# End of the attention: the first tile's rows split two batches sooner, the first product's chunks spread from the last batch's steps 6 and 7 on, Wo loaded a batch sooner

## The chip, the cores and the metric

One core of one Trainium2 chip runs the whole program in one launch. The metric is the device time of that core in microseconds (us), the median over several runs. The kernel before has 1077.09 us (three runs, 1075.11 to 1077.19).

## What is computed

Cut to what matters here (32 batches, 32 query rows and 257 context rows each, width 1024, 32 heads that share 8 key and value heads):

```
x = x + xattn(layernorm(x), context, context, Wq, Wk, Wv, Wo)   # softmax(q k^T / sqrt(32)) v, then @ Wo
x = x + attn(layernorm(x), eta)                                  # within a batch, 32 x 32
x = x + ffn(layernorm(x), gate_w, expert_w)                      # 8 experts, the best 2 of each row
```

Everything is float32. The large products run on TensorE with operands split into a high and a low part; three passes (high*high, high*low, low*high) are added.

## The kernel before

The program has two parts, `attend` and `finish`. In each of them every engine has its own list of instructions, written out by hand, and engines wait for each other by semaphores. There is no planner: the order in which the loops emit the work is the order on each engine. The names: PE is TensorE, ACT ScalarE, DVE VectorE, POOL GpSimd, SP the queue that issues most DMAs.

`attend` runs B + 2 = 34 stages `b` of 8 steps `s`. Three batches overlap: in stage b the keys and values of batch b are projected (`keys` L713, `values` L722), the heads of batch b - 1 are scored (L850), and the last heads of batch b - 2 are finished. A step works on one group of heads. PE makes the scores; DVE takes the maximum (L631); ACT takes the exponentials (L485); DVE takes the reciprocal and scales (L621, L623); two steps later PE turns the shares (`turn_prob`, L761, for the eighth head also L763); ACT or DVE, by a list (`turned_by_scalar`), copies them out of PSUM (L272). There is one PSUM buffer for turned shares, so each turn waits for the copy before it. In step 2 PE multiplies the shares of batch b - 2 by the values (`times_values`, L780), and in step 3 ACT copies the result into `oT` (L502). `oT` holds 8 tiles, each of 4 batches, turned as the product with Wo needs it; the first tile is complete once batch 3 is.

The projections of batch 31 end in step (31, 5). From step (31, 6) on there is nothing to project: these are the short steps, (31, 6) to (33, 3). There PE also makes the first tile's product with Wo, one chunk of 128 rows at a time (`first_product`, L750, six matmuls of 512 columns; steps from `product_step`). A chunk needs both parts of its Wo chunk: ACT makes the high part (L516) in the step of `wo_step`, DVE the low part (L653) one step later. It also needs both parts of the first tile's rows: ACT L520 in step (32, 1), DVE L658 in step (32, 2). The same two lines split the second tile's rows in step (33, 4). The parts lie in `rows`, where keys and shares of batch 30 lay before; thus the waits for `s_done` and `turned`.

SP loads Wo chunks 0 to 2 before stage 28, chunks 3 to 6 after the loop over the stages (they take the place of the context's parts of batch 30, so SP waits for `v_done`), chunk 7 and the two tiles of x for `finish` (L350) behind them. In every stage it stores the keys (L332) and loads them back in another layout (`kcat`, L338). The parts of chunks 3 to 6 take the place of the key and value weights, so ACT waits for the last values.

`finish` starts on each engine as soon as its part of `attend` is over. SP waits for the last `times_values` (`pv_done`), loads the gate four times (L1029, packets of 32 bytes), eta, and the eight chunks of the first expert (L1019). ACT splits the rows of tile 2 (`ot_high`, L1215), then the first expert chunk (`first_high`, L1248), then copies the turned y of tile 0 (`copy_y`, L1222). PE makes the product of tile 1 (`product`, L1546, eight units) with turns of y (L1558) before unit 4 and the small products of rows (`products_of_rows`, L1570) before unit 6; the latter wait for `copy_y`. DVE adds x to the product (`add_x`, L1330), which frees the two banks for the next tile. POOL writes constants first, once `pv_done` is reached.

The lists that the diff changes:

```
wo_step:      ((B - 2, 2), (B - 2, 6), (B - 1, 2), (B, 4), (B, 6), (B + 1, 0), (B + 1, 1), (B + 1, 2))[c]
product_step: ((B, 3), (B, 4), (B, 5), (B, 6), (B + 1, 0), (B + 1, 1), (B + 1, 2), (B + 1, 3))[c]
```

Of the kernel before, what the change touches and what calls it, by code (L numbers as in the profile page):

```python
# [12 lines left out]
ALU = mybir.AluOpType  # L13
ACT = mybir.ActivationFunctionType
# [6 lines left out]
P = 128  # L21
# [33 lines left out]
class Shared:  # L55


    def __init__(self, nc, ctx):
        sb = lambda *a: ctx.enter_context(nc.sbuf_tensor(*a))
        self.sem = sem = lambda n: ctx.enter_context(nc.semaphore(n))  # L60
        self.ident = sb("ident", [P, P], F32)
        self.base = base = nc.sbuf_base
        sb("shared_map", [P, 4 * SLOT + 4 * D], F32)
        self.at = lambda name, offset, shape, dtype=F32: nc.alloc_sbuf_tensor_at(name, shape, dtype, offset=base + offset)
        self.wkv = [self.at("wkv_" + part, HIGH1 + i * SLOT_BYTES // 2, [P, KC, 2 * KV], F32R) for i, part in enumerate("hl")]
        self.cx = self.at("cx", STAGE, [P, 2, 2, D])
        self.oT = self.at("oT", HIGH0, [P, NT, KC, P])
        place = lambda c: LOW1 + 8 * D * (c + 1) if c < EARLY_WO else LOW1 if c == KC - 1 else HIGH1 + 8 * D * (c - EARLY_WO)
        self.wo = [[self.at(f"wo_{part}{c}", place(c) + i * 4 * D, [P, D], F32R) for c in range(KC)] for i, part in enumerate("hl")]
        self.rows = [self.at("rows_" + part, STAGE + 16 * D + ROWS_AT + i * 8 * D, [P, 2, D], F32R) for i, part in enumerate("hl")]  # L70
        self.ot = [part[:, :, :].rearrange("p a (c n) -> p a c n", n=P) for part in self.rows]
        self.x_in2 = self.at("x_in2", STAGE, [P, 2, D])
        self.x2_loaded = [sem("x2_loaded0"), sem("x2_loaded1")]
        self.ot_h_ready, self.ot_l_ready, self.xo_done = sem("ot_h_ready"), sem("ot_l_ready"), sem("xo_done")
        self.w = [self.at("w_h", HIGH0, [P, 2 * SLOT], F32R), self.at("w_l", LOW0, [P, 2 * SLOT], F32R)]
        self.banks = [ctx.enter_context(nc.psum_tensor(f"bank{i}", [P, 512], F32)) for i in range(8)]

        self.chunk_loaded = [sem(f"chunk_loaded{c}") for c in range(KC)]
        self.s_done, self.pv_done = sem("s_done"), sem("pv_done")
        self.block = ctx.enter_context(nc.Block(no_gpsimd_drain=True))  # L80
        self.cx_loaded = [sem("cx_loaded0"), sem("cx_loaded1")]
# [79 lines left out]

def wo_step(c):

    return ((B - 2, 2), (B - 2, 6), (B - 1, 2), (B, 4), (B, 6), (B + 1, 0), (B + 1, 1), (B + 1, 2))[c]


def product_step(c):

    return ((B, 3), (B, 4), (B, 5), (B, 6), (B + 1, 0), (B + 1, 1), (B + 1, 2), (B + 1, 3))[c]


def attend(nc, sh, x, wq, wk, wv, wo, context, q_dram, k_dram, vlast_dram):
# [4 lines left out]
    with ExitStack() as ctx:  # L177
# [97 lines left out]
        def _(sp):  # L275
# [44 lines left out]
            def load_wo(c):  # L320
                sp.dma_start(wo_raw[c][:, :], wo[c * P:(c + 1) * P, :]).then_inc(chunk_loaded[c], 16)

            for b in range(B):
                par = b % 2
                if b == B - 4:
                    for c in range(EARLY_WO):
                        load_wo(c)
                load_context(b)
                sp.wait_ge(klast_ready, 2 * b + 2)
                for part, ready in enumerate((kT_h_ready, kT_l_ready)):  # L330
                    sp.wait_ge(ready, b + 1)
                    sp.dma_start(k_dram[part, par], kT[part][:, par, :, :].rearrange("p j n -> p (j n)").bitcast(F32)).then_inc(k_stored[part], 16)  # L332
                if b >= 2:
                    sp.wait_ge(s_done, NG * (b - 1))
                for part in range(2):
                    sp.wait_ge(k_stored[part], 16 * b + 16)
                    for c in (part, part + 2):
                        sp.dma_start(kcat[par][c * DH:(c + 1) * DH, :, :].rearrange("d (g j) n -> d g (j n)", g=4).bitcast(F32),  # L338
                                     k_dram[part, par].rearrange("(g d) n -> d g n", g=4)).then_inc(kcat_loaded[par], 16)
                if b == 0:  # L340
                    store_q(3)
            sp.wait_ge(v_done, B - 1)
            for c in range(EARLY_WO, KC - 1):
                load_wo(c)
            for part in range(2):
                sp.wait_ge(k_stored[part], 16 * B)
            load_wo(KC - 1)
# [59 lines left out]
        def _(act):  # L407
# [67 lines left out]
            for b in range(STEPS):  # L475
                project, next_one, heads, rest = stage(b)
                par = b % 2
                for s in range(NG):
# [30 lines left out]
                    for c in range(KC):  # L509
                        if wo_step(c) == (b, s):  # L510
# [3 lines left out]
                                act.wait_ge(k_stored[0], 16 * B)  # L514
                            act.wait_ge(chunk_loaded[c], 32)
                            act.activation(wo_s[0][c][:, :], wo_raw[c][:, :], ACT.Copy).then_inc(wo_h_ready, 1)  # L516
                    if (b, s) in ((B, 1), (B + 1, 4)):
                        t = b - B
                        act.wait_ge(s_done, NG * (B - 1))
                        act.activation(sh.ot[0][:, t, :, :], oT[:, t, :, :], ACT.Copy).then_inc(sh.ot_h_ready, 1)  # L520

        @block.vector
        def _(dve):
# [101 lines left out]
            for b in range(STEPS):  # L625
                project, next_one, heads, rest = stage(b)
                par = b % 2
                for s in range(NG):
                    if heads:
                        dve.wait_ge(s_done, NG * (b - 1) + s + 1)  # L630
                        dve.reduce_max(nmax[:, 1 - par, s:s + 1], s_ps[s % 2][:, 0:SK], AXX, negate=True).then_inc(max_done, 1)  # L631
                    if next_one and s in (2, 4, 6):
                        context_low(b + 1, s // 2)
                    if s == 0 and 1 <= b and next_one:
                        context_low(b + 1, 0)
                    if s == 0 and rest:
                        normalize(b - 2, NG - 1)
                    if s >= 1 and heads:
                        normalize(b - 1, s - 1)
                    i = (s - 2) % NG  # L640
                    a = b - 2 if s < 2 else b - 1
                    if s == 2 and project:
                        if b >= 2:
                            dve.wait_ge(k_stored[1], 16 * b - 16)
                        dve.wait_ge(kT_h_ready, b + 1)
                        dve.tensor_tensor(kT[1][:, par, :, 0:2 * P], k_ps[:, :].rearrange("p (j n) -> p j n", j=2),
                                          kT[0][:, par, :, 0:2 * P].bitcast(F32), ALU.subtract).then_inc(kT_l_ready, 1)
                    if i not in turned_by_scalar(a) and (rest if s < 2 else heads):
                        copy_turned(dve, dve.tensor_copy, a, i)
                    for c in range(KC):  # L650
                        if wo_step(c) == (b, s - 1):
                            dve.wait_ge(wo_h_ready, c + 1)
                            dve.tensor_tensor(wo_s[1][c][:, :], wo_raw[c][:, :], wo_s[0][c][:, :].bitcast(F32), ALU.subtract).then_inc(wo_l_ready, 1)  # L653
                    if (b, s) in ((B, 2), (B + 1, 4)):
                        t = b - B
                        dve.wait_ge(turned, NG * (B - 1))
                        dve.wait_ge(sh.ot_h_ready, t + 1)
                        dve.tensor_tensor(sh.ot[1][:, t, :, :], oT[:, t, :, :], sh.ot[0][:, t, :, :].bitcast(F32), ALU.subtract).then_inc(sh.ot_l_ready, 1)  # L658

        @block.tensor  # L660
        def _(pe):
# [80 lines left out]
            def first_product(k):  # L742

                if k == 0:
                    pe.wait_ge(sh.ot_l_ready, 1)
                    pe.wait_ge(cT_l_ready, 4 * B)
                pe.wait_ge(wo_l_ready, k + 1)
                for h in range(2):
                    for m, (a, b) in enumerate(PASSES):
                        o = pe.matmul(banks[h][:, :], sh.ot[a][:, 0, k, :], wo_s[b][k][:, h * 512:(h + 1) * 512],  # L750
                                      start=(k == 0 and m == 0), stop=(k == KC - 1 and m == 2))
                    if k == KC - 1:
                        o.then_inc(sh.xo_done, 1)
# [129 lines left out]
def finish(nc, sh, x, eta, gate, expert_w, out, n_dram, slot_dram):  # L883
# [6 lines left out]
    with ExitStack() as ctx:  # L890
# [320 lines left out]
        def _(act):  # L1211
# [29 lines left out]
            def first_high(e, *chunks):  # L1241
                for c in chunks:
                    if e == 0:
                        act.wait_ge(ot_l_ready, c + 1)
                    else:
                        act.wait_ge(xo_done, 2 * NT)
                    act.wait_ge(chunk_loaded[c], 48 + 16 * e)
                    act.activation(w[0][:, e * SLOT + c * D:e * SLOT + (c + 1) * D], first_raw[e][:, c, :], ACT.Copy).then_inc(w_h_ready, 1)  # L1248
# [498 lines left out]
```

## Time and profile before

| | |
|---|---|
| median of three runs | 1077.09 us (1075.11 to 1077.19) |
| the profiled execution, its own time | 1080.17 us |
| its span | 1078.6 us |
| PE, PE weight load, DVE, ACT, POOL busy | 97%, 89%, 58%, 44%, 23% |
| granted TensorE clock, mean over the span | 0.991 |
| HBM read, written | 148.66 MB, 44.56 MB |

Times within the profile count from the start of the span. A matmul's row shows when it starts and how long it takes from its start to its last result; matmuls overlap, so the pace is the distance from start to start. In brackets stands how long the engine was idle before the row, and what ended it. A granted clock of 1.00 is 2.4 GHz, one of 0.50 is 1.2 GHz.

### The profile page before, as it was taken

The numbers are of one execution on the slowest core, as the hardware profiler recorded it, in microseconds if no ns is written. First come the engines' busy times: TensorE is split into PE (matmuls) and PEld (weight loads), VectorE is DVE, ScalarE is ACT, GpSimd is POOL, SyncE is SP. The second block draws the span as 40 slices with busy tenths as digits, with TensorE's granted clock in tenths as the row PEclk, the third lists the DMA queues.
The fourth block names the chain that finished last, engine by engine and source line by source line (L and its number), as shares of the span: only waits on it lengthen the run. The fifth ranks groups of instructions, "written<-read, shape, count | busy, mean of one in ns | idle before, by whom it ended". The sixth has DMA issues, their size and how long they took to land.

```text
span 1078.6 us, 25384 instructions
## 1 busy us (share of the span) xinstructions
PE 1048.2 (97%) x9043; PEld 957.5 (89%) x9044; DVE 630.6 (58%) x1623; ACT 478.4 (44%) x1129; POOL 243.1 (23%) x412
## 2 busy tenths in 40 slices
PE   8999999999999999999999999799998999999996
PEld 8999999999999999999999998677776778888885
DVE  6641366666666666676766667677778344354220
ACT  4321255555555555555555555522324244454331
POOL 2000212121212111121212121035454223322232
PEclk9999999999999999999999999899998999999999
DMA  9424576566565657575757745365536677578332
GB/s 345 138 79 155 179 243 191 175 181 181 175 197 170 200 164 205 153 213 157 197 161 197 232 145 150 129 240 82 105 128 235 179 231 260 143 242 259 94 77 38
DMA packets 78604, 189.46 MB, mean 176 GB/s; under 512 B 16513, under 2 KB 27137, under 8 KB 74401
## 3 DMA queue, kind: packets, MB, share of 16 engines
q1 hardware_dynamic: 64096, 154.15, 45.7%
q0 software_dynamic: 14400, 33.88, 12.9%
q8 instruction: 69, 1.13, 0.5%
q14 instruction: 39, 0.31, 0.1%
HBM read 148.66 MB, written 44.56 MB: 179 GB/s over the span
## 4 chain that ended last, share of the span: by engine, by line
PE 89%; DMA 5%; DVE 3%; issue 1%; ACT 1%; POOL 1%; POOLq 0%; SPq 0%; DVEq 0%; ACTq 0%
PE bank L1700 17%; PE bank L713 17%; PE bank L722 16%; PE bank L674 9%; PE bank L1546 6%; PE bank L761 6%; PE bank L705 5%; PE bank L780 4%; PE bank L850 3%; DMA xg<-n_scratch,idx 1%; PE bank L1607 1%; PE bank L1580 1%; DMA out_x<-acc,idx 1%; PE bank L1616 1%; PE bank L750 1%
## 5 line engine op out<-in xcount | busy, mean ns | idle before, releaser
L485 ACT ACTIVATE prob<-bank,nmax 128x257 f32<-128x257 f32 x256 | 122.1, 477 | 239.9 <-DVE nmax L631 239.9
L631 DVE TENSOR_REDUCE nmax<-bank 128x1 f32<-128x257 f32 x256 | 108.9, 425 | 155.9 <-PE bank L850 155.9
L722 PE MATMUL bank<-wkv_h,cT_h 128*128 128x256 f32 x512 | 154.5, 302 | 0.0
L713 PE MATMUL bank<-cT_h,wkv_h 128*128 128x256 f32 x512 | 154.3, 301 | 0.0
L722 PE MATMUL bank<-wkv_h,cT_l 128*128 128x256 f32 x512 | 144.6, 282 | 0.0
L713 PE MATMUL bank<-cT_h,wkv_l 128*128 128x256 f32 x512 | 144.3, 282 | 0.0
L722 PE MATMUL bank<-wkv_l,cT_h 128*128 128x256 f32 x512 | 144.1, 281 | 0.0
L713 PE MATMUL bank<-cT_l,wkv_h 128*128 128x256 f32 x512 | 144.0, 281 | 0.0
L380 POOL DMA_DIRECT2D qcat<-q_scratch x128 | 70.5, 557 | 271.5 <-PE bank L850 268.4
L1700 PE MATMUL bank<-w_h,rows_h 128*128 x272 | 108.7, 400 | 0.0
L1700 PE MATMUL bank<-w_l,rows_h 128*128 x272 | 107.3, 394 | 0.0
L1700 PE MATMUL bank<-w_h,rows_l 128*128 x272 | 107.3, 394 | 0.0
L761 PE MATMUL bank<-ident,prob 128*128 128x128 f32 x512 | 100.1, 277 | 3.9 <-DVE pT L272 2.8
L1444 DVE TENSOR_TENSOR rows_l<-bank,rows_h 128x512 fp32r<-128x512 f32 x42 | 27.0, 683 | 126.4 <-ACT rows_h L1257 114.2
L722 PEld LDWEIGHTS bank<-wkv_h,cT_h 128*128 128x128 f32 x512 | 97.3, 190 | 0.0
L623 DVE TENSOR_SCALAR prob<-prob,rsums 128x257 f32<-128x257 f32 x256 | 92.0, 359 | 9.1
L713 PEld LDWEIGHTS bank<-cT_l,wkv_h 128*128 128x128 f32 x512 | 97.2, 190 | 0.0
L722 PEld LDWEIGHTS bank<-wkv_l,cT_h 128*128 128x128 f32 x512 | 97.1, 190 | 0.0
L713 PEld LDWEIGHTS bank<-cT_h,wkv_h 128*128 128x128 f32 x512 | 96.9, 189 | 0.0
L713 PEld LDWEIGHTS bank<-cT_h,wkv_l 128*128 128x128 f32 x512 | 96.8, 189 | 0.0
L722 PEld LDWEIGHTS bank<-wkv_h,cT_l 128*128 128x128 f32 x512 | 96.7, 189 | 0.0
L565 DVE TENSOR_TENSOR cT_l<-bank,cT_h 128x512 fp32r<-128x512 f32 x128 | 87.1, 682 | 10.1 <-ACT cT_h L440 10.1
(211 smaller groups left out, 2377.8 us busy)
## 6 DMA issues: line engine op xcount, KB each, us to landing
kcat<-k_scratch SPq DMA_DIRECT2D x128, 258.0 KB, 4.2
cx<-in_context SPq DMA_DIRECT2D x32, 1024.0 KB, 7.1
raw<-in_expert_w SPq DMA_DIRECT2D x48, 512.0 KB, 7.5
qcat<-q_scratch POOLq DMA_DIRECT2D x128, 128.0 KB, 3.1
k_scratch<-kT_h SPq DMA_DIRECT2D x32, 258.0 KB, 2.5
k_scratch<-kT_l SPq DMA_DIRECT2D x32, 258.0 KB, 2.5
x_in<-in_x SPq DMA_DIRECT2D x16, 512.0 KB, 9.2
expert_raw<-in_expert_w SPq DMA_DIRECT2D x16, 512.0 KB, 8.3
```

The source lines that it names most:

```text
L380: pool.dma_start(qcat[c * DH:(c + 1) * DH, par, :, :].rearrange("d (g j) n -> d g (j n)", g=4).bitcast(F32), q_dram[c // 2, b].rearrange(" ...
L485: act.activation(prob[1 - par][:, s, 0:SK], s_ps[s % 2][:, 0:SK], ACT.Exp, bias=nmax[:, 1 - par, s:s + 1], accum_out=sums[:, 1 - par, s:s ...
L565: dve.tensor_tensor(cT[1][:, b % 2, 2 * m:2 * m + 2, :].rearrange("p a n -> p (a n)"), cT_ps[m % 2][:, :], high, ALU.subtract).then_inc(cT ...
L623: dve.tensor_scalar(prob[a % 2][:, i, 0:SK], prob[a % 2][:, i, 0:SK], rsums[:, i:i + 1], None, ALU.mult).then_inc(prob_ready, 1)
L631: dve.reduce_max(nmax[:, 1 - par, s:s + 1], s_ps[s % 2][:, 0:SK], AXX, negate=True).then_inc(max_done, 1)
L674: o = pe.matmul(q_ps(UNITS * g + u)[:, m % 2 * GT:(m % 2 + 1) * GT], wq_s[w][:, k, m * P:(m + 1) * P], xT[g % 2][t][:, k, :], start=(m % 2 ...
L705: o = pe.transpose(cT_ps[m % 2][:, n * P:(n + 1) * P], cx[:, b % 2, a, k * P:(k + 1) * P], ident[:, :])
L713: o = pe.matmul(k_ps[:, j * 256:(j + 1) * 256], wkv[w][:, k, j * P:(j + 1) * P], cT[t][:, b % 2, k, :], start=(j == 0 and k == 0 and n == ...
L722: o = pe.matmul(v_ps[:, a * KV:(a + 1) * KV], cT[t][:, b % 2, k, a * P:(a + 1) * P], wkv[w][:, k, KV:2 * KV], start=(a == 0 and k == 0 and ...
L761: o = pe.transpose(turn_ps[:, c * P:(c + 1) * P], prob[a % 2][:, i, c * P:(c + 1) * P], ident[:, :])
L1546: o = pe.matmul(o_ps[h][:, :], ot[a][:, t % 2, k, :], wo_s[b][k][:, h * 512:(h + 1) * 512], start=(k == 0 and m == 0), stop=(k == KC - 1 a ...
L1700: o = pe.matmul(y_ps[par][h][:, :], gT[a][:, par, k * P:(k + 1) * P], w[b][:, bass.ds(slot_at + (k * D + h * 512), 512)], start=(k == 0 an ...
```

## The change

The steps of the splits of Wo chunks 3 to 7 move ahead: chunk 3 to (31, 6), 4 to (32, 0), 5 to (32, 2), 6 to (32, 4), 7 to (32, 6). The products go to (31, 6), (31, 7), (32, 0), (32, 1), (32, 3), (32, 5), (32, 7) and (33, 1). SP loads chunks 3 to 6 at the head of stage 31, ahead of the store of batch 31's keys. The first tile's rows are split at (30, 7) on ACT and (31, 0) on DVE, into places of their own: the high part where context rows of batch 31 lay, once they are all turned, the low part over the first tile of `oT` itself. The second tile's rows are split at (33, 0) instead of (33, 4), and, as before, into `rows`. In `finish` ACT waits for the first tile's product before it writes the first expert's high part over that low part.

```diff
@@ Shared @@
+        self.ot_first = [self.at("ot_first_h", STAGE + 12 * D, [P, KC, P], F32R), self.at("ot_first_l", HIGH0, [P, KC, P], F32R)]
@@ wo_step, product_step @@
-    return ((B - 2, 2), (B - 2, 6), (B - 1, 2), (B, 4), (B, 6), (B + 1, 0), (B + 1, 1), (B + 1, 2))[c]
+    return ((B - 2, 2), (B - 2, 6), (B - 1, 2), (B - 1, 6), (B, 0), (B, 2), (B, 4), (B, 6))[c]
-    return ((B, 3), (B, 4), (B, 5), (B, 6), (B + 1, 0), (B + 1, 1), (B + 1, 2), (B + 1, 3))[c]
+    return ((B - 1, 6), (B - 1, 7), (B, 0), (B, 1), (B, 3), (B, 5), (B, 7), (B + 1, 1))[c]
@@ SP @@
+                if b == B - 1:
+                    sp.wait_ge(v_done, B - 1)
+                    for c in range(EARLY_WO, KC - 1):
+                        load_wo(c)
                 load_context(b)
...
-            sp.wait_ge(v_done, B - 1)
-            for c in range(EARLY_WO, KC - 1):
-                load_wo(c)
@@ ACT @@
-                    if (b, s) in ((B, 1), (B + 1, 4)):
-                        t = b - B
+                    if (b, s) == (B - 2, 7):
+                        act.wait_ge(cT_done, 4 * B)
+                        act.activation(sh.ot_first[0][:, :, :], oT[:, 0, :, :], ACT.Copy).then_inc(sh.ot_h_ready, 1)
+                    if (b, s) == (B + 1, 0):
                         act.wait_ge(s_done, NG * (B - 1))
-                        act.activation(sh.ot[0][:, t, :, :], oT[:, t, :, :], ACT.Copy).then_inc(sh.ot_h_ready, 1)
+                        act.activation(sh.ot[0][:, 1, :, :], oT[:, 1, :, :], ACT.Copy).then_inc(sh.ot_h_ready, 1)
@@ DVE @@
-                    if (b, s) in ((B, 2), (B + 1, 4)):
-                        t = b - B
+                    if (b, s) == (B - 1, 0):
+                        dve.wait_ge(sh.ot_h_ready, 1)
+                        dve.tensor_tensor(sh.ot_first[1][:, :, :], oT[:, 0, :, :], sh.ot_first[0][:, :, :].bitcast(F32), ALU.subtract).then_inc(sh.ot_l_ready, 1)
+                    if (b, s) == (B + 1, 0):
                         dve.wait_ge(turned, NG * (B - 1))
-                        dve.wait_ge(sh.ot_h_ready, t + 1)
+                        dve.wait_ge(sh.ot_h_ready, 2)
...
@@ PE, first_product @@
-                        o = pe.matmul(banks[h][:, :], sh.ot[a][:, 0, k, :], wo_s[b][k][:, h * 512:(h + 1) * 512],
+                        o = pe.matmul(banks[h][:, :], sh.ot_first[a][:, k, :], wo_s[b][k][:, h * 512:(h + 1) * 512],
@@ finish, ACT, first_high @@
                     if e == 0:
+                        if c == 0:
+                            act.wait_ge(xo_done, 2)
                         act.wait_ge(ot_l_ready, c + 1)
```

## Rows read from the trace of the kernel before

**Rows 1.** Windows of 20 us across the end of the attention: busy time by engine, PEclk

```profile
660.00:680.00 20.00, 16.09 (x177) 14.55 (x179) 13.09 (x42) 10.82 (x33) 0.53 (x1) 0.86 0.70 227
680.00:700.00 20.00, 16.64 (x136) 12.45 (x129) 12.57 (x26) 11.00 (x24) 1.28 (x11) 0.97 0.15 55
700.00:720.00 20.00, 19.50 (x146) 14.94 (x145) 12.72 (x26) 5.48 (x8) 8.76 (x15) 1.00 0.82 274
```

**Rows 2.** Waits from 655 to 705 us, the largest of PE's

```profile
PE bank L761 <- DVE pT L272: 2.5, 3, 1.2
```

**Rows 3.** Timeline of PE from step (30, 6) into tile 1, some rows

```profile
655.41 0.28 PE L850 MATMUL bank<-kcat,qcat 128*128 128x258 f32 x1
...
671.23 0.28 PE L850 MATMUL bank<-kcat,qcat 128*128 128x258 f32 x1
...
674.99 0.55 PE L850 MATMUL bank<-kcat,qcat 128*128 128x258 f32 x1 [1.59 <-issue]
...
684.92 0.29 PE L850 MATMUL bank<-kcat,qcat 128*128 128x258 f32 x1
...
686.64 0.28 PE L850 MATMUL bank<-kcat,qcat 128*128 128x258 f32 x1
...
692.22 0.41 PE L761 MATMUL bank<-ident,prob 128*128 128x128 f32 x2 [1.18 <-DVE pT L272]
...
697.05 0.65 PE L780 MATMUL bank<-pT,v_sb 128*32 128x128 f32 x16
...
698.50 0.50 PE L750 MATMUL bank<-wo_h,rows_h 128*128 128x512 f32 x1
...
702.05 0.47 PE L1546 MATMUL bank<-wo_h,rows_h 128*128 128x512 f32 x1 [0.50 <-DVE x L1330]
...
711.44 0.80 PE L1570 MATMUL bank<-yT 128*32 128x40 f32 x64
```

**Rows 4.** Windows of half a microsecond at the edges of the low clock (PEclk: third from last)

```profile
674.50:675.00 0.50, 0.01 (x1) 0.04 (x1) 0.00 (x0) 0.00 (x0) 0.00 (x0) 0.54 0.97 385
681.00:681.50 0.50, 0.50 (x11) 0.30 (x3) 0.00 (x0) 0.00 (x0) 0.00 (x0) 0.64 1.03 410
...
828.00:828.50 0.50, 0.32 (x2) 0.32 (x2) 0.34 (x3) 0.42 (x2) 0.20 (x1) 0.64 0.88 107
834.50:835.00 0.50, 0.50 (x3) 0.40 (x2) 0.10 (x1) 0.00 (x0) 0.00 (x0) 0.54 0.00 0
```

**Rows 5.** Timeline of DVE over one head with a split behind it

```profile
690.86 0.43 DVE L631 TENSOR_REDUCE nmax<-bank 128x1 f32<-128x257 f32 x1 [1.08 <-PE bank L850]
...
691.39 0.36 DVE L623 TENSOR_SCALAR prob<-prob,rsums 128x257 f32<-128x257 f32 x1
691.66 0.42 DVE L272 COPY pT<-bank 128x256 f32<-128x256 f32 x1
691.99 1.22 DVE L653 TENSOR_TENSOR wo_l<-wo_raw,wo_h 128x1024 fp32r<-128x1024 f32 x1
693.12 0.16 DVE L621 RECIPROCAL rsums<-sums 128x1 f32<-128x1 f32 x1
```

**Rows 6.** Timeline of SP's queue: the last keys, and the first loads of `finish`

```profile
667.76 1.74 SPq L338 DMA_DIRECT2D kcat<-k_scratch  x4
...
698.63 2.29 SPq L1029 DMA_DIRECT2D yT<-in_gate  x4
...
702.06 5.08 SPq L1019 DMA_DIRECT2D expert_raw<-in_expert_w  x8
```

**Rows 7.** Timeline of ACT: the first expert chunk and the copies of y

```profile
708.03 1.06 ACT L1248 ACTIVATE w_h<-expert_raw 128x1024 fp32r<-128x1024 f32 x1 [5.39 <-DMA expert_raw<-in_expert_w]
709.00 1.07 ACT L1222 ACTIVATE yT<-bank 128x512 f32<-128x512 f32 x2
```

**Rows 8.** Loads of x (L1016, L350): time from issue to landing, 512 KB each

```profile
DMA to landing us min/median/max: 3.6/9.6/11.8
```

**Rows 9.** Timeline of PE: the wait ahead of the later fall of the clock

```profile
828.18 0.59 PE L1590 MATMUL bank<-both,earlier 128*128 128x8 f32 x2 [2.06 <-DVE both L1387]
```

More of the change, by code:

```diff
@@ L653, in _ @@
                             dve.tensor_tensor(wo_s[1][c][:, :], wo_raw[c][:, :], wo_s[0][c][:, :].bitcast(F32), ALU.subtract).then_inc(wo_l_ready, 1)
-                    if (b, s) in ((B, 2), (B + 1, 4)):
-                        t = b - B
+                    if (b, s) == (B - 1, 0):
+                        dve.wait_ge(sh.ot_h_ready, 1)
+                        dve.tensor_tensor(sh.ot_first[1][:, :, :], oT[:, 0, :, :], sh.ot_first[0][:, :, :].bitcast(F32), ALU.subtract).then_inc(sh.ot_l_ready, 1)
+                    if (b, s) == (B + 1, 0):
                         dve.wait_ge(turned, NG * (B - 1))
-                        dve.wait_ge(sh.ot_h_ready, t + 1)
-                        dve.tensor_tensor(sh.ot[1][:, t, :, :], oT[:, t, :, :], sh.ot[0][:, t, :, :].bitcast(F32), ALU.subtract).then_inc(sh.ot_l_ready, 1)
+                        dve.wait_ge(sh.ot_h_ready, 2)
+                        dve.tensor_tensor(sh.ot[1][:, 1, :, :], oT[:, 1, :, :], sh.ot[0][:, 1, :, :].bitcast(F32), ALU.subtract).then_inc(sh.ot_l_ready, 1)
         @block.tensor
```

## The prediction

> **What bounds the kernel now.** The page shows PE busy for 97% of the span, so I looked for the stretches where it is not. In the windows of 20 us [rows 1] PE is idle for 3.9 us, 3.4 us and 0.5 us from 660 to 720. The waits [rows 2] give the largest kind there, turns of the shares that wait for DVE's copy of the turn before (2.5 us). The timeline of PE [rows 3] gives the longest single one, 1.59 us at the first score of stage 32, which no engine released; it needs the keys that SP loads back last (a DMA). The third loss is the clock: the granted clock goes to 0.50 (1.2 GHz) between 674.5 and about 681.3 [rows 4]. All of it lies in the short steps, from the score of step (31, 6) at 671.23 to the first matmul of tile 1 at 702.05 [rows 3], 30.8 us.
>
> **What that stretch holds.** A step with a chunk of the product takes 1.72 us from score to score at full clock (684.92 to 686.64), and the shares times values 1.45 (697.05 to 698.50) [rows 3]. Of the 1.72 I put 0.12 on the score, 0.22 on the turn, 1.38 on the chunk. Ten scores, twelve turns, two small ones at 0.11, eight chunks and two times values are 1.2 + 2.6 + 0.2 + 11.0 + 2.9 = 18.0 us. So 12.8 of the 30.8 us are waits and half clock, and the change can only win from these; the 18.0 stay.
>
> **The change, part by part.**
>
> *Rows of the first tile, (30, 7) and (31, 0).* The split is moved, not removed. ACT has room at (30, 7). On DVE it takes as long as the low part of a Wo chunk, 1.13 us from start to start [rows 5], and stands ahead of the maximum of (31, 1). The exponential and the last two copies of batch 29 follow on ACT, and the times values of batch 29 wait for these. Walked in the order of the lists they come 0.3 us after PE is ready for them. Bounds: 0 (DVE catches up) and 1.1 (nothing hidden). I take 0.3 late, nearest to the walk, since DVE idles in most steps of this stage.
>
> *Wo chunks 3 to 6 loaded at the head of stage 31.* Batch 30's values are done at score (30, 6), 655.4 [rows 3]. There SP can issue, 12 us ahead of its loads of the last keys (667.76 [rows 6]). 2 MB at the 410 GB/s of a full stretch [rows 4] take 5.1 us; with issue and latency I allow 664, and ACT's first use is at 673.6 by the walk below. Behind the key loads now stand chunk 7 and two tiles of x, 1.5 MB, instead of 3.5. The keys land no later than now, so score (32, 0) can start at 675.0 [rows 3] or sooner. Between nothing and 1.0 us (stores of keys that meet the end of the Wo loads) I take nothing: two chunks on PE cover it.
>
> *Chunks 0 and 1 in (31, 6) and (31, 7).* Score (31, 6) at 671.6, two steps of 1.72, so score (32, 0) at 675.05: the 1.59 us wait for the keys and the waits beside it are filled with work, and the fall of the clock that followed them should go.
>
> *Chunks 2 and 3.* (32, 0) takes 1.72, (32, 1) 1.72, 0.11 for the small turn and 0.4 of waiting, as DVE is behind with the low part of chunk 3: score (32, 2) at 679.1. Times values of batch 30, turn and score: (32, 3) at 680.9.
>
> *Steps (32, 3) to (33, 1).* Now one chunk comes to every two heads, and its low part is DVE work. Per two heads DVE has two maxima with reciprocals (0.53 each), two scalings (0.27), one copy (0.33) and one low part (1.13) [rows 5], 3.06 us in all, while PE has 2 x 0.34 + 1.38 = 2.06. So DVE sets the pace. With 0.2 where DVE waits for a score or for ACT's high part, a pair takes 3.3 us. The chunk of (32, 3) has no wait for its low part, as that is 3 steps old. Walk: score (32, 3) 680.9, (32, 5) 683.7, (32, 7) 687.0; turn and chunk 6 to 690.1; the eighth head's turn waits 0.9 behind the low part of chunk 7 and the scaling, chunk 7 runs 691.5 to 692.9. Waits of PE by this walk: 0.4, 0.8, 1.3, 1.4 and 0.9, together 4.9 us (before: 12.8). Times values of batch 31 start at 692.95 instead of 697.05 [rows 3], 4.1 us sooner.
>
> *Tile 1.* Both parts of its rows are split in (33, 0) and ready before 693.3, and DVE's addition for the first bank comes during the times values. So the wait of 0.50 us and the two chunks behind the times values go: tile 1 starts at 694.5, not 702.05, 7.5 us sooner (12.8 - 4.9 - 0.3 = 7.6 by the other count).
>
> *What is late next.* SP's first load of `finish` stays tied to the end of the last times values: 1.58 us after their start, at 698.63, now 694.5. From there everything to the copies of y keeps its length: 3.43 us to the first expert chunk's issue [rows 6], 5.97 to its landing, 2.04 for ACT's split and the two copies of y behind it [rows 7], 11.44 in all. PE needs y 9.39 us after tile 1's start (702.05 to 711.44 [rows 3]). Before, tile 1 started 3.42 us after that first load, so PE came 1.4 us after the copies. Now both start at 694.5: PE comes at 703.9 and waits until 705.95, **a new wait of 2.1 us**. POOL's constants and the third tile of x are tied to the last times values in the same way and come 1.4 us or more nearer to their use; before, no wait of PE named either, and I cost them at nothing. If that cover is too thin, tile 0's y is late by what is missing, but under the same new wait. ACT's added wait for the first product costs nothing: the split ahead of it already waits for the same count.
>
> From the products of rows on all engines stand to each other as before. **Sum: 711.44 - 705.95 = 5.5 us** (7.5 gained, 2.1 given back). The profiled execution took 1080.17 us, so 1074.7 on its scale; it was 3.1 us longer than the median, and against the median 1077.09 - 5.5 = **1071.6**.
>
> **Rivals.**
>
> *The expert chunk lands sooner, no new wait.* Its 5.97 us stand behind the gate's small packets and beside seven other chunks. A load of the same size with nothing beside it landed in 3.6 us [rows 8]. Then the copies are done after 9.1 us, ahead of PE, and the whole 7.5 us stay: 1069.6. Against it: the same loads are issued in the same order and nothing else is in the queue, before or after. 10%.
> The Trainium skill (DMA: Bandwidth & Descriptors, Anatomy of one DMA) gives a fixed 2.0 us plus bytes over 436 GB/s for a DMA issued by GpSimd, by which 512 KB would be an estimated 3.2 us and the wait would go too. The trace disagrees for this chunk (5.97 us), and I go by the trace.
>
> *The new wait makes the clock fall.* A wait of 2.06 us with full work on both sides stood ahead of the fall at 828.2 [rows 9], which lasted to about 835 [rows 4]. Both falls lasted some 6.8 us at half pace, 3.4 us of work. The new wait is as long, and tile 1 is PE bound: 5.5 - 3.4 = 2.1 gained, 1075.0. For it: that row. Against it: 1.18 us of waiting at 692.2 [rows 3], with more just before and behind it, left the clock at 1.00, so the edge is somewhere between; it may well differ from run to run. 27%.
>
> *The clock falls in the short steps.* PE waits up to 1.4 us in each pair. Half pace for 6.8 us doubles some 4 us of work, part of it in the waits: 2.5 to 3.4 late, about 1074.5. The steps at 688 to 695 look alike and kept the clock. 7%.
>
> *Slower: the splits line up with the softmax.* Five splits now stand among the last heads' steps, before two of them. If ACT's high part and DVE's low part each held up the chain of every head in turn, a split would cost up to 0.96 + 1.13 = 2.1 us. Eight steps of 1.72 from 675.05 end at 688.8; with 5 x 2.1 and 2.5 for the last turns and chunk 7 the times values start at 701.8, 4.8 later than now, and 1.4 comes back as above: 3.4 slower, 1080.5. It decides from 1.4 us for each split on. Against it: the step from 690.86 holds a head and a split in 2.26 us of DVE [rows 5], ACT is idle in over a third of the window from 680 on [rows 1], and the heads overlap. 5%.
>
> *It does nothing*, since the waits only move behind the later heads: 3%, 1077.
>
> **How the numbers follow.** Forecast 48%, the cases above 10, 27, 7, 5 and 3. About 0.2%, or 2.15 us, is what a measurement can tell. The range reaches from the first rival to the two with a fallen clock, with 0.3 and 1.0 for the walk: 1069.3 to 1076.0. Faster: forecast, no new wait, and nearly two thirds of the fallen clock cases, which lie at the bound: 0.78. Within 0.2%: 0.16. Slower: 0.06.
>
> **What would show it.** Right: chunks 0 and 1 on PE at about 671.9 and 673.6, score (32, 0) without a wait, granted clock 1.00 from 660 to 700; turns of (32, 3), (32, 5), (32, 7) each waiting about a microsecond for copies; last times values near 693, tile 1 right behind them; the products of rows waiting near 2 us for ACT's copies of y, themselves behind the expert chunk. Wrong: a score (32, 0) later than 676, a first tile that waits for Wo parts, tile 1 later than 696.5, or a granted clock under 1.00 from 704 on.

## The result and the profile after

The changed kernel takes 1074.95 us (median of 20 runs, 1073.71 to 1078.92), the kernel before 1078.06 us (20 runs, 1075.11 to 1081.74). The ratio is 0.9975, 95% interval 0.9967 to 0.9983: 2.7 us faster, with an interval from 1.8 to 3.6 us. The forecast was 5.5 us. The changed kernel's profiled execution took 1077.07 us, its span is 1075.4 us.

The windows of 20 us after the change, as in [rows 1]. The profiled execution reached step (30, 6) at 654.74, the one before at 655.41, so at the same time on the axis it is 0.67 us further on in the work.

```profile
660.00:680.00 20.00, 18.86 (x190) 16.81 (x192) 15.40 (x41) 10.74 (x33) 0.53 (x1) 1.00 0.81 238
680.00:700.00 20.00, 16.64 (x150) 13.12 (x141) 15.20 (x33) 10.16 (x25) 4.97 (x20) 1.00 0.14 12
700.00:720.00 20.00, 17.73 (x137) 13.69 (x136) 10.33 (x30) 4.75 (x8) 7.01 (x10) 0.91 0.76 289
```

From 660 to 680 PE idles 1.1 us instead of 3.9, and the clock keeps at 1.00. But from 700 to 720, where PE was nearly always busy, it idles 2.3 us instead of 0.5, and the granted clock is down to 0.91.

The timeline of PE, the rows that answer to [rows 3]: the scores of (31, 6), (31, 7), (32, 0) to (32, 3), (32, 5) and (32, 7), the last times values, tile 1, the first products of rows (other rows are left out).

```profile
670.77 0.28 PE L856 MATMUL bank<-kcat,qcat 128*128 128x258 f32 x1
672.57 0.28 PE L856 MATMUL bank<-kcat,qcat 128*128 128x258 f32 x1
675.46 0.35 PE L856 MATMUL bank<-kcat,qcat 128*128 128x258 f32 x1 [0.99 <-issue]
677.26 0.28 PE L856 MATMUL bank<-kcat,qcat 128*128 128x258 f32 x1
679.10 0.28 PE L856 MATMUL bank<-kcat,qcat 128*128 128x258 f32 x1
680.95 0.37 PE L856 MATMUL bank<-kcat,qcat 128*128 128x258 f32 x1
683.76 0.36 PE L856 MATMUL bank<-kcat,qcat 128*128 128x258 f32 x1
687.08 0.36 PE L856 MATMUL bank<-kcat,qcat 128*128 128x258 f32 x1
...
693.06 0.64 PE L786 MATMUL bank<-pT,v_sb 128*32 128x128 f32 x16
...
694.50 0.50 PE L1554 MATMUL bank<-wo_h,rows_h 128*128 128x512 f32 x1
...
706.28 0.80 PE L1578 MATMUL bank<-yT 128*32 128x40 f32 x64 [2.27 <-ACT yT L1228]
```

Chunks 0 and 1 fill the two steps from 670.77, yet score (32, 0) still waits 0.99 us. From (32, 5) to (32, 7) two heads take 3.3 us (683.76 to 687.08), as worked out. Tile 1 starts 7.55 us earlier than before; 0.67 of it was there ahead of the change, so 6.9 us come of it. The new wait is there, 2.27 us.

What follows is easiest to read in distances from the score of step (30, 6), since executions differ by up to a microsecond before it. All from the timeline of PE:

| us after score (30, 6) | before | changed | chunk first | Wo halved | both | three chunks | rows only |
|---|---|---|---|---|---|---|---|
| score (32, 0) | 19.58 | 20.72 | 21.87 | 19.63 | 19.54 | 20.00 | 19.65 |
| last times values | 41.64 | 38.32 | 39.48 | 37.45 | 37.46 | 42.08 | 42.42 |
| first products of rows | 56.03 | 51.54 | 50.37 | 51.17 | 48.35 | 56.20 | 56.54 |
| second products of rows | 71.40 | 68.44 | 65.71 | 67.82 | 63.68 | 71.57 | 71.89 |

From the second products of rows up to the last tiles the two timelines run in parallel (61.33 us to the sixth in both), so this last row is what the changed stretch is worth: 2.96 us, near the measured 2.7. Behind it both executions have their own waits and falls of the clock.

### The profile page after: what moved, and what is told of

The parts are those of the page before. It is cut to its first block, busy times and chain, and to the rows that moved or that the text cites. A ratio compares the mean times of both kernels' runs of the same rounds, so it can differ in the third digit from the quotient of the medians.

```text
span 1075.4 us, 25383 instructions
## 1 busy us (share of the span) xinstructions
PE 1046.3 (97%) x9043; PEld 957.9 (89%) x9044; DVE 630.2 (59%) x1623; ACT 477.4 (44%) x1129; POOL 242.3 (23%) x412
## 3 DMA queue, kind: packets, MB, share of 16 engines
q8 instruction: 69, 1.13, 0.5%
## 4 chain that ended last, share of the span: by engine, by line
PE 90%; DMA 3%; DVE 3%; issue 2%; POOL 1%; ACT 1%; SPq 0%; POOLq 0%; DVEq 0%; ACTq 0%
PE bank L1708 18%; PE bank L728 17%; PE bank L719 17%; PE bank L680 9%; PE bank L1554 6%; PE bank L767 6%; PE bank L711 5%; PE bank L786 4%; PE bank L856 3%; PE bank L1615 2%; PE bank L1624 1%; DMA xg<-n_scratch,idx 1%; DMA expert_raw<-in_expert_w 1%; PE bank L756 1%; PE bank L1588 1%
```

## Two waits and a fall of the clock, read from the changed kernel

SP's queue: Wo, the store of the last keys, their loads; then the first loads of `finish`.

```profile
654.94 2.79 SPq L322 DMA_DIRECT2D wo_raw<-in_wo  x4
663.99 0.33 SPq L337 DMA_DIRECT2D k_scratch<-kT_h  x1
664.74 0.33 SPq L337 DMA_DIRECT2D k_scratch<-kT_l  x1
669.05 1.74 SPq L343 DMA_DIRECT2D kcat<-k_scratch  x4
...
694.64 2.90 SPq L1035 DMA_DIRECT2D yT<-in_gate  x4
...
698.68 4.43 SPq L1025 DMA_DIRECT2D expert_raw<-in_expert_w  x8
```

The loads of the last keys wait for their stores, which are issued at 663.99 and 664.74. They are issued 14.3 us after the score of (30, 6), before it was 12.35 (667.76 less 655.41, [rows 3, 6]). DMA was busy where it had been free:

```profile
661.00:663.00 2.00, 1.89 (x17) 1.66 (x15) 1.93 (x7) 0.99 (x5) 0.00 (x0) 1.00 1.02 283
663.00:665.00 2.00, 1.96 (x53) 1.76 (x53) 0.92 (x2) 1.86 (x4) 0.12 (x1) 1.00 1.02 226
665.00:667.00 2.00, 2.00 (x19) 2.00 (x18) 1.59 (x5) 0.74 (x3) 0.41 (x1) 1.00 0.96 290
```

The second number from the right is the DMA share, about 1 right up to 667, where the 2 MB issued from 654.94 on should have been gone by 664.

ACT, then the granted clock behind the new wait:

```profile
704.20 1.06 ACT L1256 ACTIVATE w_h<-expert_raw 128x1024 fp32r<-128x1024 f32 x1 [8.22 <-DMA expert_raw<-in_expert_w]
705.16 1.07 ACT L1228 ACTIVATE yT<-bank 128x512 f32<-128x512 f32 x2
```

```profile
706.00:708.00 2.00, 1.72 (x67) 1.46 (x68) 1.43 (x4) 0.61 (x3) 0.00 (x0) 0.81 1.03 422
708.00:710.00 2.00, 2.00 (x7) 1.52 (x5) 1.15 (x8) 0.00 (x0) 0.00 (x0) 0.50 1.02 418
710.00:712.00 2.00, 2.00 (x9) 1.64 (x8) 0.27 (x1) 0.34 (x1) 0.00 (x0) 0.84 1.03 410
```

ACT sits idle for 8.2 us until the expert chunk lands. y had been turned long before (PE L1566 starts at 700.19 and takes 1.03 us), but its copy stands behind the chunk's split. From 707.2, 1 us after PE's wait, the clock is at its lower level (1.2 GHz). From the first to the second products of rows it takes 16.90 us, before 15.37.

## Experiments

**The first expert chunk ahead of the gate.** Edit, in SP's part of `finish`:

```diff
+            sp.wait_ge(xo_done, 2)
+            load_first(0, 0)
             sp.wait_ge(sh.pv_done, B)
...
-            sp.wait_ge(xo_done, 2)
-            for c in range(KC):
+            for c in range(1, KC):
                 load_first(0, c)
```

> The changed kernel, but SP issues the first expert's chunk 0 as soon as the first product is done, ahead of the gate's loads. Theory: the 2.27 us wait at the first products of rows stands behind that chunk, which ACT splits before it copies y; then the wait goes (under 0.3 us), the granted clock stays at 1.00 from 700 to 715, and the time falls by 2.3 + 1.5 = 3.8 us against the changed kernel, some 6 to 7 against the kernel before. Rival (y itself is late, behind POOL's constants): the wait stays near 2 us and so does the time. Rival (what is gained here is given back at the last tiles' gather): the wait goes, but the time falls by less than 1.5 us.

Measured: 1072.43 us, ratio to the kernel before 0.9949 (0.993 to 0.9967), 5.5 us faster (3.6 to 7.6), a little under the 6 to 7 expected. No wait at the first products of rows, clock 1.00 from 660 to 840. The stretch to the second products of rows lost 1.16 us at score (32, 0), where this execution waited 2.15 us, and still came out 2.73 us ahead of the changed kernel (table). So the repair is worth 2.73 + 1.16 = 3.9 us in the traces, one execution of each kernel, as the theory had it. In the ratios to the kernel before the two kernels differ by 2.8 us, with wide intervals. The ACT row shows why: y is copied as soon as it is turned, and the first expert chunk is no longer in front.

```profile
702.19 1.09 ACT L1229 ACTIVATE yT<-bank 128x512 f32<-128x512 f32 x2 [3.11 <-PE bank L1567]
```

**y copied first, loads as they were.** Edit, in ACT's loop of `finish`:

```diff
+                if t == 1:
+                    copy_y(0)
                 if 1 <= t < NT:
                     first_high(0, t - 1)
...
-                if on(t, 1):
+                if on(t, 1) and t > 1:
                     copy_y(t - 1)
```

> The changed kernel, but ACT copies the turned y of tile 0 before it splits the first expert chunk. Theory (ACT's order and the chunk): the wait at the first products of rows is gone, with loads as they were, as in the kernel with the chunk first: 3.8 us less than the changed kernel. Rival (the DMA traffic of that stretch or POOL's constants hold PE): the wait stays over 1.5 us.

Measured: 1074.32 us, ratio 0.9949 (0.9934 to 0.9965), 5.5 us faster than before; that is 2.8 us less than the changed kernel by the ratios, where 3.8 were expected. ACT, then PE:

```profile
703.70 1.09 ACT L1228 ACTIVATE yT<-bank 128x512 f32<-128x512 f32 x2 [4.85 <-PE bank L1568]
...
708.00 1.06 ACT L1256 ACTIVATE w_h<-expert_raw 128x1024 fp32r<-128x1024 f32 x1 [3.22 <-DMA expert_raw<-in_expert_w]
```

```profile
706.82 0.80 PE L1580 MATMUL bank<-yT 128*32 128x40 f32 x64
```

The wait is gone with the loads unchanged, so neither DMA traffic nor POOL held PE; it was the order on ACT. This execution waited 2.14 us at score (32, 0) and its clock fell there (0.50 from 678 to 680), which cost it 1.6 us more by the last times values (41.05 after score (30, 6), chunk first 39.48). From the first to the second products of rows it took 16.05 us instead of 16.90, of which 0.45 is a wait for DVE's addition of x, which now stands behind the later expert chunk. So this repair moves part of the wait to DVE; the other one doesn't.

**Work in the wait.** Nine matmuls ahead of the first products of rows, whose result isn't used:

```diff
             def products_of_rows(t):
+                if t == 0:
+                    for _ in range(9):
+                        pe.matmul(r_ps[0][:, :], ot[0][:, 1, 0, :], wo_s[0][0][:, 0:512], start=True, stop=True)
```

> The changed kernel with nine matmuls of 512 columns put ahead of the first products of rows, whose result nobody reads (2.1 us of work at full clock in the place of the wait). Theory (idle PE makes the clock fall there, in this execution and in most): wait under 0.4 us, the products of rows start when they did, 11.6 us after SP's first load of the second part, the clock stays at 1.00 there and PE is 1.5 us earlier one tile on; the time falls by 1.5 us at most, by less where other executions did not fall. Rival (the fall at 707 has nothing to do with the wait): clock falls all the same, time unchanged or up.

Measured: 1076.65 us, ratio 0.9984 (0.997 to 0.9999). The wait is 0.20 us, and the clock stays up:

```profile
707.98 0.80 PE L1581 MATMUL bank<-yT 128*32 128x40 f32 x64 [0.20 <-ACT yT L1228]
```

```profile
706.00:708.00 2.00, 1.80 (x11) 1.15 (x10) 1.01 (x1) 1.93 (x3) 0.00 (x0) 1.00 1.02 418
708.00:710.00 2.00, 2.00 (x70) 1.73 (x71) 1.41 (x6) 0.38 (x2) 0.00 (x0) 1.00 1.02 420
```

From the first to the second products of rows it takes 15.34 us, against 16.90. So idle PE brought the fall, and in the changed kernel's profiled execution the fall costs 1.56 us. The total did not follow: by the ratios it is no lower than the changed kernel's. This execution waited 1.96 us at score (32, 0) and 4.01 us for the gather at 845.87, where the changed kernel waited 2.92. What makes the total higher than the local gain says is not settled.

**Half of Wo behind the last keys.**

```diff
                 if b == B - 1:
                     sp.wait_ge(v_done, B - 1)
-                    for c in range(EARLY_WO, KC - 1):
+                    for c in (3, 4):
                         load_wo(c)
...
+            for c in (5, 6):
+                load_wo(c)
             for part in range(2):
                 sp.wait_ge(k_stored[part], 16 * B)
```

> The changed kernel with Wo chunks 5 and 6 loaded behind the last keys, only 3 and 4 at the head of stage 31. Theory (2 MB of Wo hold up the store of the last keys, 5 us instead of 3): the key loads are issued by 3.5 us after the high keys' store, 1.5 us sooner, and the 0.99 us wait at the first score of stage 32 is gone; 1.0 us less than the changed kernel, 1.0 still lost nowhere else. Rival (key loads are late for another reason): the wait stays at 1.0. Rival (the wait is hidden anyway, DVE sets the pace of the short steps): it goes, and tile 1 starts no sooner.

Measured: 1075.54 us, ratio 0.9969 (0.9955 to 0.9983). The total can't be told from the changed kernel's, so the 1.0 us expected doesn't show in it. SP's queue, PE at score (32, 0), and DMA:

```profile
664.02 0.33 SPq L337 DMA_DIRECT2D k_scratch<-kT_h  x1
664.77 0.83 SPq L337 DMA_DIRECT2D k_scratch<-kT_l  x1
666.95 1.74 SPq L343 DMA_DIRECT2D kcat<-k_scratch  x4
```

```profile
674.41 0.36 PE L858 MATMUL bank<-kcat,qcat 128*128 128x258 f32 x1
```

```profile
663.00:665.00 2.00, 1.93 (x52) 1.73 (x53) 0.95 (x2) 1.90 (x5) 0.09 (x1) 1.00 0.10 34
```

The keys' loads leave 2.1 us sooner than in the changed kernel, DMA is at 0.10 when the store begins, and no wait is left at score (32, 0), 19.63 instead of 20.72. The last times values come 0.87 us sooner. So the 2 MB of Wo held up the store, and that reached PE. Only 0.37 of it arrives at the first products of rows, since the new wait grew to 2.76 us: the expert chunk's issue came 4.27 us after SP's first load of `finish` (4.04 in the changed kernel) and its landing 5.79 us after that (5.52). At the second products of rows 0.62 us are left. The next experiment takes that wait away.

**Both repairs.** The edits of the first and the fourth experiment together.

> The changed kernel with both repairs: the first expert's chunk 0 loaded ahead of the gate, and Wo chunks 5 and 6 loaded behind the last keys. Theory: no wait at the first score of stage 32, none at the first products of rows, clock at 1.00 from 660 to 715; the second products of rows come 63.7 us after the score of step (30, 6) (before 71.4, changed 68.4, chunk first 65.7), so 7.7 us less than before up to there, and some 6 to 7.5 us less in all. Rival (the gather at the end takes it back): the anchor comes as said and the time falls by less than 5.

Measured: **1070.12 us** (6 runs, 1069.15 to 1073.35), ratio 0.9927 (0.9913 to 0.994), 7.9 us faster than before. The second products of rows come at 63.68, to the expected 63.7.

```profile
660.00:680.00 20.00, 19.66 (x202) 17.69 (x204) 16.26 (x45) 11.16 (x33) 0.53 (x1) 1.00 0.80 250
680.00:700.00 20.00, 16.64 (x143) 13.01 (x136) 15.69 (x33) 10.90 (x26) 5.17 (x20) 1.00 0.24 41
700.00:720.00 20.00, 20.00 (x216) 15.72 (x215) 14.26 (x41) 5.87 (x10) 7.79 (x10) 1.00 0.73 286
```

PE idles 0.3, 3.4 and 0.0 us; the 3.4 are the waits for copies and for DVE's last scaling in the pairs. It is faster than the kernel before and the changed one. Against the kernel with the chunk first, the second products come 2.03 us sooner: without the new wait the earlier keys do reach the end of the stretch.

**The kernel before, y first.** The edit of the second experiment on the kernel before.

> The kernel before, with ACT's copies of tile 0's y put ahead of the split of the first expert chunk. Theory (the wait is made by tile 1 starting beside SP's loads; before the change PE came 1.4 us after the copies): no change, within 0.2%. Rival (the order cost the kernel before too): 1 us or more faster.

Measured: 1079.07 us, ratio 1.0004 (0.9991 to 1.0016). The order on ACT cost the kernel before nothing; the change turned it into a wait.

**Three chunks only.** Wo loads and `wo_step` of the kernel before, and

```diff
-    return ((B - 1, 6), (B - 1, 7), (B, 0), (B, 1), (B, 3), (B, 5), (B, 7), (B + 1, 1))[c]
+    return ((B - 1, 6), (B - 1, 7), (B, 0), (B, 6), (B + 1, 0), (B + 1, 1), (B + 1, 2), (B + 1, 3))[c]
```

> Of the change only the early split of both tiles' rows and chunks 0 to 2 of the product at (31, 6), (31, 7), (32, 0); Wo loads, splits and products 3 to 7 as before. Theory (half of the gain is the empty stretch at 672 to 682 and its clock, the other half the later splits out of the tail): no fall of the clock before 700, last times values 39.6 us after the score of (30, 6) instead of 41.6, tile 1 at 44.5 instead of 46.6, where the change has 38.3 and 39.8; 2 us of gain, and since tile 1 starts behind two chunks no new wait at the products of rows. Rival (the filled stretch is the whole gain): tile 1 at 41 or sooner.

Measured: 1079.17 us, ratio 1.0009 (0.9997 to 1.0021). Both expectations missed: the last times values came at 42.08, later than before. The emptied steps (32, 1) to (32, 5) have too little for PE, and the clock falls there instead:

```profile
680.00:682.00 2.00, 0.78 (x6) 0.54 (x6) 1.83 (x7) 1.11 (x5) 0.00 (x0) 1.00 0.84 334
682.00:684.00 2.00, 1.09 (x6) 0.62 (x5) 1.71 (x6) 2.00 (x7) 0.00 (x0) 0.79 0.07 20
684.00:686.00 2.00, 1.73 (x5) 1.32 (x6) 1.48 (x4) 1.03 (x5) 0.00 (x0) 0.50 0.00 0
...
692.00:694.00 2.00, 1.73 (x7) 1.05 (x5) 1.45 (x2) 0.62 (x2) 0.00 (x0) 0.65 0.00 0
```

No single wait from 675 to 690 was over 1.1 us. From 680 to 685 there were four of 0.55 to 0.66 us, three of them ahead of the fall, which begins at 683.2 and lasts 10.2 us. Filling the hole at 672 alone moves the fall.

**Rows only.** As the last, with the products too where they were.

> Of the change only the early split of both tiles' rows; all products, Wo loads and splits as before. Theory: the first chunk's wait of 0.63 us goes, the split of the second tile now stands ahead of Wo parts on ACT and DVE and gives that back: tile 1 at 46.8 us after the score of (30, 6) (before 46.6), clock falls at 674 as before, time within 0.2% of before. Rival (waits for the rows' split were the bound): 1 us or more faster.

Measured: 1080.29 us, ratio 1.0017 (1.0008 to 1.0025), a little slower. The last times values come 0.78 us later than before: chunk 5 waits 2.35 us for its low part, as ACT and DVE now split tile 1's rows between Wo parts. The wait at score (32, 0) is 1.46 us and the clock falls later and for half as long (3.4 us from 677.3, expected was 674 as before), and it still isn't faster. The early split of the rows is a condition of the rest and no gain by itself.

**Two more executions of the changed kernel.**

> The changed kernel once more, for its trace. Theory: again a wait of 2.2 to 2.8 us at the first products of rows with a fall of the clock behind it, and a wait of 0.9 to 2.2 us at the first score of stage 32; the second products of rows 68.4 to 69.6 us after the score of step (30, 6). Rival (the fall was this one execution's): a clock of 1.00 from 700 to 715 and the second products of rows 1.5 us sooner than the two waits make them.

> The changed kernel a third time, with the same two theories: a fall of the clock behind the wait at the first products of rows in every execution, or in some.

Measured: 1075.12 and 1075.68 us. Waits of 1.68 and 1.74 us at score (32, 0), of 2.31 and 2.71 us at the first products of rows, second products at 68.93 and 69.44. The clock fell at the second wait in both, and in the kernel with halved Wo too: four of the four executions that had this wait, none of the four whose wait was removed or filled (chunk first, y first, work in the wait, both). Each fall lasted 3.4 us at the lower level. It began 1 us after the wait's end in the first execution and 0.4 us before it in the other three. From the first to the second products of rows these three take 16.66, 16.67 and 16.65 us, 1.3 more than the 15.34 at full clock.

## Why the prediction was wrong

The direction was right and the time lies in the range given, but the gain was put at twice its size: 5.5 us forecast, 2.7 measured (3.1 by the two medians). By its own steps:

- *Work against waits, 18.0 and 12.8 us.* Right. In the kernel with halved Wo, which has none of the DMA trouble, the last times values come 37.45 us after the score of (30, 6); the walk said 692.95 less 655.41, 37.54. Its waits for the copies, and the last one for DVE's scaling, are 0.56, 1.06, 1.13 and 0.61 us, forecast 0.8, 1.3, 1.4 and 0.9. The 0.4 forecast ahead of chunk 3 is hardly there: step (32, 1) takes 2.05 us instead of 2.23.
- *DVE sets the pace, 3.3 us for two heads.* Right, 3.32 measured, in which DVE idles for 0.2 us.
- ***Wo at the head of stage 31 costs nothing.*** This failed. I named the meeting with the store of the keys and bounded it at 1.0 us, then took nothing, since two chunks were to cover it. The 5.1 us for 2 MB left out that the same DMA engines also carry the queries' loads (0.5 MB), which POOL issues at 657.09 in the changed kernel's timeline, and the store met the end of both. The rate was too high as well: with the DMA share at about 1 the windows from 661 to 667 moved 283, 226 and 290 GB/s, not the 410 of one window of half a microsecond. The stores took 5.0 and 4.9 us to land, with only half of Wo ahead of them 2.9 and 3.1. The wait was 0.99, 1.68 and 1.74 us in the three executions of the changed kernel, and 2.15, 2.14 and 1.96 in the other three with these loads, beyond the bound of 1.0 in all but one: some 1.5 us of the missing 2.8.
- *The new wait, 2.1 us.* Right in place, cause and almost in size: 2.27, 2.31 and 2.71 us.
- ***The clock behind that wait.*** The likeliest case had it at 1.00; the rival with the fall, at 27%, is what happens every time. Its price was mis-sized: 3.4 us came from falls of 6.8 us, these last half as long and cost 1.3 to 1.56 us. My own row of a 2.06 us wait with a fall behind it [rows 9] was the nearest one; the weight belonged on that side.
- *The third tile of x and POOL's constants cost nothing.* Right. DVE waited 1.51 us for POOL before y (1.03 before), under the same new wait; nothing reached PE.

5.5 less some 1.5 for the keys, 1.5 for the clock and 0.3 for the longer wait is 2.2; measured 2.7 (1.8 to 3.6), and 2.5 in the profiled executions (3.2 less the 0.67 they differ by ahead of the change). The parts are sizes read from single executions, so the sum can't be held to better than about half a microsecond. The rivals: the splits lining up with the softmax did not happen (two heads and a split take 3.3 us), nor did the expert chunk land sooner. Its landing, 5.5 us from issue (698.68 to 704.20), stays far from the 3.2 us estimated in the prediction from the fit that the Trainium skill (DMA: Bandwidth & Descriptors, Anatomy of one DMA) gives for a DMA issued by GpSimd. Issued ahead of the gate's loads and the other chunks, the same chunk is in use 3.5 us after its issue (694.52 to 698.02, chunk first), so the other 2.0 us come with the loads ahead of it and beside it.

## What to carry to other kernels

When a change brings two engines' schedules together, look at what is tied to an event and not to the work that moved: a load issued at the end of a stage keeps its length and becomes the wait. A free queue is not a free DMA: here 2 MB of loads lengthened a store although 6 us lay between the last load's issue and the store's (657.73 to 663.99). And after a stretch is tightened, count the lone waits of about 2 us that stay in it, as each may bring the lower clock; a load issued sooner removes both.

## What the runs showed of the hardware beside this

- A single wait of 2.3 to 2.8 us between stretches of full work brought the granted clock to 0.50 in four of four executions, for 3.4 us; the falls at 674 and 828 in the kernel before lasted 6.8 us each. The wait of 2.06 to 2.08 us late in the kernel [rows 9], which every traced execution has, was followed by a fall in 5 of 12 (before, changed in two of three, y first, Wo halved). Of the waits of 1.96, 2.14 and 2.15 us at score (32, 0) only that of 2.14 was, so one such wait is a risk and no certainty. The wait of 1.70 to 1.76 us that follows 8 to 11 us after the one of 2.06 (PE at 832.19 in the changed kernel) was not, in any of the 12.
- In the kernel with three chunks only, three waits of 0.55 to 0.66 us in a row, with PE busy for 0.78 us of a window of 2 us, stood ahead of a fall too, so a stretch can lose the clock with no long wait in it.
- Late in the kernel the turn of the gathered rows waits for a chain of small DMAs. It comes 120.9 to 122.6 us after the second products of rows in all twelve executions, whether the clock fell at the wait of 2.06 us between them or not:

```profile
844.68 1.54 PE L1615 MATMUL bank<-ident,xg 128*128 128x128 f32 x6 [2.92 <-DMA xg<-n_scratch,idx]
```

  In the kernel before a fall of the clock at 828 lay in the shadow of that wait (0.26 us were left of it), in the changed one the wait was 2.92 us and a fall of 6.8 us began in it, at 843.8. With work in the wait and with half of Wo the gather came 1.0 us later after the second products than in the changed kernel (122.55 and 122.50 against 121.50), which may be part of why their totals don't follow the local gains; why it came later is open. So single executions differ there by over a microsecond either way, and local distances tell more than one total.
